# The last stage of a four-layer graph network: column sums by TensorE, squares and the row norm by ScalarE, rows in three parts, stores in five

## What is computed

```python
def _layernorm(x, axis=-1, eps=1e-05):
    m = jnp.mean(x, axis=axis, keepdims=True)
    v = jnp.var(x, axis=axis, keepdims=True)
    return (x - m) / jnp.sqrt(v + eps)
...
        agg = jax.ops.segment_sum(msg, dst, num_segments=h.shape[0])
        mean = jnp.mean(agg, axis=0)
        var = jnp.mean(jnp.square(agg - mean), axis=0)
        out = (agg - mean) * jax.lax.rsqrt(var + BN_EPS) * gamma + beta
        return out
...
    x = _layernorm(x + _L3_gnn_ref(x, L3_gnn_weight, L3_gnn_gamma, L3_gnn_beta, src, dst, edge_type_8), axis=-1)
```

## Time and profile before

| | us |
|---|---|
| three timed runs | 6064.71, 6073.38, 6078.59; median 6073.38 |
| the profiled execution: time | 6069.67 |
| its span, from the first to the last instruction | 6067.9 |
| busy in the span: PE 65%, DVE 57%, POOL 50%, PEld 50%, ACT 31% | |
| `batch_norm_out`: first VectorE instruction to the end of the span | 5971.09 to 6067.9 |

### The profile page before, as it was taken

One profiled execution on the slowest core, in us unless ns is written; L12 is line 12 of the kernel. 1 busy time (PEld: TensorE's weight loads), 2 busy tenths in 40 slices (PEclk: granted clock), 3 DMA queues, 4 the chain that ended last, 5 costly groups with the idle time before them and its releaser, 6 DMA issues. The chain is left out here.

```text
span 6067.9 us, 60178 instructions
## 1 busy us (share of the span) xinstructions
PE 3945.1 (65%) x16761; PEld 3027.2 (50%) x16761; DVE 3476.9 (57%) x6672; ACT 1868.0 (31%) x3951; POOL 3020.3 (50%) x3023
## 2 busy tenths in 40 slices
PE   1665566663966666657666667977667689945551
PEld 1564355551445555544455556855555567533331
DVE  8898544446845445466566666546666653222225
ACT  0002412213842222224445453425455443200000
POOL 3686666657763555511455552125555521066661
PEclk9656777776976777769788888988888889976776
DMA  1242244452022333333555654135556632233333
GB/s 43 62 99 51 73 116 116 114 100 52 3 45 71 100 98 97 100 71 129 156 163 172 171 163 104 38 118 169 172 165 169 158 96 79 102 96 91 94 93 48
DMA packets 281671, 630.50 MB, mean 104 GB/s; under 512 B 71500, under 2 KB 126128, under 8 KB 278192
## 3 DMA queue, kind: packets, MB, share of 16 engines
q0 software_dynamic: 159168, 436.21, 28.1%
q1 hardware_dynamic: 122224, 190.89, 10.2%
HBM read 560.35 MB, written 65.91 MB: 103 GB/s over the span
## 5 line engine op out<-in xcount | busy, mean ns | idle before, releaser
L1005 PE MATMUL edge_sums<-edge_rows,edge_hot 128*128 128x272 f32 (+2 forms) x3712 | 1182.1, 480 | 626.7 <-issue 347.0
L938 POOL DMA_INDIRECT edge_rows<-kv_rows,dst_index x928 | 879.1, 947 | 1042.0 <-PE edge_sums L1005 379.4
L1005 PEld LDWEIGHTS edge_sums<-edge_rows,edge_hot 128*128 128x128 f32 x3712 | 863.8, 241 | 882.8 <-issue 565.2
L1015 DVE TENSOR_TENSOR l_acc<-l_acc,edge_sums 128x272 f32 (+2 forms) x928 | 394.4, 425 | 557.5 <-remote 248.9
L938 POOL DMA_INDIRECT begun_rows<-xl_rows,dst_index x464 | 441.4, 951 | 434.6 <-PE edge_sums L1005 243.2
L1084 DVE TENSOR_TENSOR edge_rows<-edge_own_rows,edge_rows 128x1024 f32<-128x1024 f32 x232 | 282.6, 1218 | 545.9 <-DMA table_dst<-front_dst_stage_all 261.2
L938 POOL DMA_INDIRECT edge_rows<-rel_rows,dst_other_index x464 | 439.5, 947 | 308.2 <-issue 130.8
L1269 PE MATMUL edge_own_rows<-dst_x,edge_hot_t 128*128 x1856 | 545.3, 447 | 31.6 <-ACT edge_hot_t L969 21.2
L938 POOL DMA_INDIRECT edge_rows<-rows,src_index x464 | 439.6, 947 | 243.2 <-issue 132.7
L207 POOL DMA_INDIRECT table_src<-src_src_stage_all x333 | 415.9, 1249 | 158.0 <-issue 99.9
L1269 PEld LDWEIGHTS edge_own_rows<-dst_x,edge_hot_t 128*128 128x128 f32 x1856 | 413.8, 229 | 106.3 <-issue 34.9
(11 more groups left out here) (447 smaller groups left out, 7468.6 us busy)
## 6 DMA issues: line engine op xcount, KB each, us to landing
edge_where<-local_dst SPq DMA_DIRECT2D x174, 256.0 KB
dst_rank_keys<-in_dst SPq DMA_DIRECT2D x85, 312.5 KB
rel_rows<-nodes_out SPq DMA_DIRECT2D x25, 1024.0 KB
edge_where<-local_src SPq DMA_DIRECT2D x58, 256.0 KB
edge_rows<-kv_rows,dst_index POOLq DMA_INDIRECT x928
kv_rows<-nodes_out SPq DMA_DIRECT2D x50, 260.0 KB, 2.1
edge_rows<-rows,src_index POOLq DMA_INDIRECT x464
begun_rows<-xl_rows,dst_index POOLq DMA_INDIRECT x464
```

Of the source, the lines that this page charges most:

```text
L938: pool.indirect_dma_start(out=self.rows[:, h * U + b, 0:self.width], out_offset=None, in_=self.source[:, :], in_offset=bass.IndirectOffset ...
L1005: last = nc.tensor.matmul(sums[p % len(sums)][:, 0:width], self.hot[s % 2][:, 2 * (p % 4) + i, :], self.half(s)[:, 2 * (p % 4) + i, first: ...
L1015: nc.vector.tensor_tensor(into, into, sums[p % len(sums)][:, 0:width], ALU.add).then_inc(stored, 1)
```

## The change

Every part of `batch_norm_out` is rewritten; the rest of the program keeps its instructions and their order.

- **Sum over nodes.** VectorE adds tiles 0 to 7 and 8 to 15 into eight, then these into four tiles of `sq`. TensorE multiplies ones by tiles 16 to 24 of `acc` one by one and by those four, all 13 accumulating in one bank, `total0`.
- **Bias early.** `x + b` over all 25 tiles is done while TensorE sums; it waits for the loads of `g` and `b`.
- **Squares.** VectorE subtracts the mean five tiles at a time; ScalarE squares each five. TensorE sums 15 tiles of squares one by one, VectorE folds the last ten into five, and TensorE adds these five, 20 matmuls in `total1`.
- **Row norm in three parts** of 10, 10 and 5 tiles: scale, residual, statistics and the small sums for one part, then ScalarE's root, then reciprocal and shift. ScalarE applies `x * scale + shift` to tiles 0 to 21; VectorE does so for tiles 22 to 24.
- **Stores** of five tiles each as soon as ScalarE has counted them off; the last five go in two transfers (four tiles, 53 rows).

```diff
@@ -2476,63 +2476,131 @@
 def batch_norm_out(nc, k, acc, x, gamma, beta, out):
+    parts = [(0, 10), (10, 20), (20, NT)]
+    shared = NT - 3
     with Phase(nc, "bn") as ph:
-        norm = Norm(ph)
         g, b = ph.sb("g", [P, C]), ph.sb("b", [P, C])
         mean, scale = ph.sb("node_mean", [P, C]), ph.sb("node_scale", [P, C])
         sq = ph.sb("sq", [P, NT, C])
-        col, total = ph.sb("col", [P, C]), ph.ps("total", [P, 2, C])
+        total = [ph.ps(f"total{n}", [P, 512]) for n in range(2)]
         pad = ph.sb("pad", [P, 1])
-        own, loaded, folded, summed, varied, rooted, ready, stored = (
-            ph.sem(n) for n in ("own", "loaded", "folded", "summed", "varied", "rooted", "ready", "stored"))
+        stats = ph.sb("stats", [P, NT, 6])
+        row_mean, row_var, row_tmp, row_scale, row_shift = (ph.sb(n, [P, NT]) for n in ("row_mean", "row_var", "row_tmp", "row_scale",
+                                                                                       "row_shift"))
+        own, loaded, folded, summed, centred, squared, paired, varied, rooted, measured, spread, row_rooted, ready = (
+            ph.sem(n) for n in ("own", "loaded", "folded", "summed", "centred", "squared", "paired", "varied", "rooted",
+                                "measured", "spread", "row_rooted", "ready"))
+        added, by_act, by_dve, stored = (ph.sem(n) for n in ("added", "by_act", "by_dve", "stored"))
         block = ph.block()
+        five = lambda n: slice(5 * n, 5 * n + 5)
         @block.sync
         def _(sp):
             sp.dma_start(g[:, :], gamma.partition_broadcast(P)).then_inc(loaded, 16)
             sp.dma_start(b[:, :], beta.partition_broadcast(P)).then_inc(loaded, 16)
-            sp.wait_ge(ready, 1)
-            full = (NT - 1) * P
-            sp.dma_start(out[0:full, :].rearrange("(t p) c -> p t c", p=P), x[:, 0:NT - 1, :]).then_inc(stored, 16)
-            sp.dma_start(out[full:N, :], x[0:NL, NT - 1, :]).then_inc(stored, 16)
-            sp.wait_ge(stored, 32)
+            for n in range(NT // 5):
+                last = 5 * n + 5
+                sp.wait_ge(by_act, min(last, shared))
+                if last < NT:
+                    sp.dma_start(out[5 * n * P:last * P, :].rearrange("(t p) c -> p t c", p=P), x[:, five(n), :]).then_inc(stored, 16)
+                    continue
+                sp.wait_ge(by_dve, NT - shared)
+                sp.dma_start(out[5 * n * P:(NT - 1) * P, :].rearrange("(t p) c -> p t c", p=P), x[:, 5 * n:NT - 1, :]).then_inc(stored, 16)
+                sp.dma_start(out[(NT - 1) * P:N, :], x[0:NL, NT - 1, :]).then_inc(stored, 16)
+            sp.wait_ge(stored, 16 * (NT // 5 + 1))
         @block.tensor
         def _(pe):
-            for n in range(2):
-                pe.wait_ge(folded, n + 1)
-                nc.tensor.matmul(total[:, n, :], k.ones[:, :], col[:, :], start=True, stop=True).then_inc(summed, 1)
+            def column_sums(n, rows, start, stop):
+                for r in range(len(rows)):
+                    last = nc.tensor.matmul(total[n][:, 0:C], k.ones[:, :], rows[r], start=start and r == 0,
+                                            stop=stop and r == len(rows) - 1)
+                return last
+            column_sums(0, [acc[:, t, :] for t in range(16, NT)], True, False)
+            pe.wait_ge(folded, 1)
+            column_sums(0, [sq[:, t, :] for t in range(4)], False, True).then_inc(summed, 1)
+            for n in range(3):
+                pe.wait_ge(squared, n + 1)
+                column_sums(1, [sq[:, t, :] for t in range(5 * n, 5 * n + 5)], n == 0, False)
+            pe.wait_ge(paired, 1)
+            column_sums(1, [sq[:, t, :] for t in range(15, 20)], False, True).then_inc(summed, 1)
         @block.scalar
         def _(act):
+            for n in range(5):
+                act.wait_ge(centred, n + 1)
+                nc.scalar.activation(sq[:, five(n), :], acc[:, five(n), :], ACT.Square).then_inc(squared, 1)
             act.wait_ge(varied, 1)
             nc.scalar.activation(scale[:, :], scale[:, :], ACT.Sqrt).then_inc(rooted, 1)
-            norm.act(nc, act)
+            for n, (first, last) in enumerate(parts):
+                act.wait_ge(spread, n + 1)
+                nc.scalar.activation(row_var[:, first:last], row_var[:, first:last], ACT.Sqrt).then_inc(row_rooted, 1)
+                act.wait_ge(ready, n + 1)
+                for t in range(first, min(last, shared)):
+                    nc.scalar.activation(x[:, t, :], x[:, t, :], ACT.Identity, bias=row_shift[:, t:t + 1],
+                                         scale=row_scale[:, t:t + 1]).then_inc(by_act, 1)
         @block.vector
         def _(dve):
             step = Chain(dve, own)
-            wide = lambda a: a[:, :].unsqueeze(1).to_broadcast([P, NT, C])
-            nc.vector.tensor_reduce(col[:, :], acc[:, :, :].rearrange("p t c -> p c t"), AX.X, ALU.add).then_inc(folded, 1)
-            step(nc.vector.tensor_scalar(pad[:, :], k.row[:, :], float(NL), None, ALU.is_lt))
+            wide = lambda a, n: a[:, :].unsqueeze(1).to_broadcast([P, n, C])
+            step(nc.vector.tensor_tensor(sq[:, 0:8, :], acc[:, 0:8, :], acc[:, 8:16, :], ALU.add))
+            nc.vector.tensor_tensor(sq[:, 0:4, :], sq[:, 0:4, :], sq[:, 4:8, :], ALU.add).then_inc(folded, 1)
+            nc.vector.tensor_scalar(pad[:, :], k.row[:, :], float(NL), None, ALU.is_lt)
+            dve.wait_ge(loaded, 32)
+            nc.vector.tensor_tensor(x[:, :, :], x[:, :, :], wide(b, NT), ALU.add).then_inc(added, 1)
             dve.wait_ge(summed, 1)
-            step(nc.vector.tensor_scalar(mean[:, :], total[:, 0, :], 1.0 / N, None, ALU.mult))
-            step(nc.vector.tensor_tensor(acc[:, :, :], acc[:, :, :], wide(mean), ALU.subtract))
-
-            step(nc.vector.tensor_scalar(acc[:, NT - 1, :], acc[:, NT - 1, :], pad[:, 0:1], None, ALU.mult))
-            step(nc.vector.tensor_tensor(sq[:, :, :], acc[:, :, :], acc[:, :, :], ALU.mult))
-            nc.vector.tensor_reduce(col[:, :], sq[:, :, :].rearrange("p t c -> p c t"), AX.X, ALU.add).then_inc(folded, 1)
+            step(nc.vector.tensor_scalar(mean[:, :], total[0][:, 0:C], 1.0 / N, None, ALU.mult))
+            for n in range(5):
+                ins = nc.vector.tensor_tensor(acc[:, five(n), :], acc[:, five(n), :], wide(mean, 5), ALU.subtract)
+                if n == 4:
+                    step(ins)
+                    ins = nc.vector.tensor_scalar(acc[:, NT - 1, :], acc[:, NT - 1, :], pad[:, 0:1], None, ALU.mult)
+                ins.then_inc(centred, 1)
+            dve.wait_ge(squared, 5)
+            nc.vector.tensor_tensor(sq[:, five(3), :], sq[:, five(3), :], sq[:, five(4), :], ALU.add).then_inc(paired, 1)
             dve.wait_ge(summed, 2)
-            nc.vector.tensor_scalar(scale[:, :], total[:, 1, :], 1.0 / N, EPS, ALU.mult, ALU.add).then_inc(varied, 1)
+            nc.vector.tensor_scalar(scale[:, :], total[1][:, 0:C], 1.0 / N, EPS, ALU.mult, ALU.add).then_inc(varied, 1)
             dve.wait_ge(rooted, 1)
             step(nc.vector.reciprocal(scale[:, :], scale[:, :]))
-            dve.wait_ge(loaded, 32)
             step(nc.vector.tensor_tensor(scale[:, :], scale[:, :], g[:, :], ALU.mult))
-            step(nc.vector.tensor_tensor(acc[:, :, :], acc[:, :, :], wide(scale), ALU.mult))
-            step(nc.vector.tensor_tensor(x[:, :, :], x[:, :, :], acc[:, :, :], ALU.add))
-            step(nc.vector.tensor_tensor(x[:, :, :], x[:, :, :], wide(b), ALU.add))
-            norm.dve(nc, dve, step, x, x)
-            nc.vector.memset(pad[:, :], 0.0).then_inc(ready, 1)
+            dve.wait_ge(centred, 5)
+            def merge(n):
+                first, last = parts[n]
+                of = slice(first, last)
+                step(nc.vector.tensor_tensor(acc[:, of, :], acc[:, of, :], wide(scale, last - first), ALU.mult))
+                if not n:
+                    dve.wait_ge(added, 1)
+                step(nc.vector.tensor_tensor(x[:, of, :], x[:, of, :], acc[:, of, :], ALU.add))
+                for t in range(first, last):
+                    nc.vector.bn_stats(stats[:, t, :], x[:, t, :]).then_inc(measured, 1)
+                dve.wait_ge(measured, last)
+                nc.vector.tensor_tensor(row_mean[:, of], stats[:, of, 1], stats[:, of, 4], ALU.add)
+                nc.vector.tensor_tensor(row_tmp[:, of], stats[:, of, 1], stats[:, of, 4], ALU.subtract)
+                step(nc.vector.tensor_tensor(row_var[:, of], stats[:, of, 2], stats[:, of, 5], ALU.add))
+                nc.vector.tensor_scalar(row_mean[:, of], row_mean[:, of], 0.5, None, ALU.mult)
+                nc.vector.scalar_tensor_tensor(row_tmp[:, of], row_tmp[:, of], 0.25, row_tmp[:, of], ALU.mult, ALU.mult)
+                step(nc.vector.tensor_scalar(row_var[:, of], row_var[:, of], 1.0 / C, EPS, ALU.mult, ALU.add))
+                nc.vector.tensor_tensor(row_var[:, of], row_var[:, of], row_tmp[:, of], ALU.add).then_inc(spread, 1)
```

(13 more changed lines are left out.)

## The result

In five timed runs each the kernel before took 6068.22 us (median; 6064.71 to 6078.59) and the changed kernel 6037.86 us (6029.31 to 6042.74). That is 30.4 us less; the ratio is 0.9945, with a 95% interval of 0.9933 to 0.9957. The forecast was 6037.0 in a range of 6028 to 6050.

A forecast was written before the change was run, and what follows sets the result against it. VectorE's chain, with nothing beside it, was taken to bound the last stage. Compute 56.8 + stores 6.3 = 63.1 us against 96.8, 33.7 less, gave 6036.0 from the profiled execution, 6039.7 from the median; forecast 6037, range 6028 to 6050.

The forecast's parts named there:

- three parts: Row norm: ten, ten and five tiles cost VectorE 28.1 us together, some 4 us more than one pass.
- first sum: Sum over nodes: TensorE's 26 records take 5.7 us, free behind the bias; the mean begins at 10.4 us.
- squares: Sum of squares: TensorE, starting at 13.75 us with 3.3 us at half clock, ends last at 24.35.
- bounds of 23.7 and 31.35: End of the squares' sum in us: 23.7 with full clock at once, 31.35 with half clock throughout.
- Rival B: TensorE at half clock throughout the squares adds 7.0 us, giving 6043; chance 0.18.
- stores: End of stage: four stores go under compute, leaving 6.3 us after the last tile, against 14.0 before from issue to end.
- C: Accumulating matmuls on ones don't overlap, each costing 1.23 us: 19.6 us more, 6056; chance 0.05.
- D: The four added stores pay 2.6 us each in turn, 10.4 us, giving 6046; chance 0.06.
- E: Moved data or code slows 2320 gathers ahead of the stage; 14.5 ns each eats the gain; no change 0.03, slower 0.03.

## Why the prediction was right

| step | predicted | measured |
|---|---|---|
| mean starts | 10.4 | 10.27 |
| subtraction and zeroing done | 18.4 | 18.20 |
| VectorE's fold done | 21.3 | 21.03 |
| column scale starts | 24.35 | 25.06 |
| three parts | 28.1 | 55.85 - 28.22 = 27.6 |
| last tile normalised | 56.8 | 56.97 |
| from there to the end | 6.3 | 6.35 |
| stage | 63.1 | 63.32 |

The **first sum** was hidden behind the bias as said, at full clock, with 4.4 us to spare. That spare was in the prediction's own numbers (5.7 against 10.4) and was called cover that "was due anyway"; the run with the bias in two pieces shows that 4 us of it could have gone elsewhere. The forecast wasn't hurt, the kernel was.

The **squares** had the right last engine and a term that was 0.7 us too small: 3.3 us at half clock were assumed and 5.2 measured, which costs 0.95, while TensorE began 0.2 earlier than summed (13.57 against 13.75). The prices of 0.43 and 0.22 us a record are a little above what the earlier trace rows gives by division (2.70/7 = 0.39, 2.20/11 = 0.20); the changed kernel has 0.40 and 0.21. The bounds of 23.7 and 31.35 held, and the lower one was met by the run with the extra matmuls (23.55). Rival B, half clock throughout, did not happen in any run.

The **three parts** cost 27.6 us, 0.5 less than the sum, about 0.15 in each: the small sums took 0.9 us for 1.0, and from the root to the next part were 0.6 for 0.7. Splitting cost 3.7 us over one pass (27.63 against 23.89 in the run with one part), where some 4 were worked out. ScalarE had 0.58 us to spare ahead of the third root, where 0.8 were worked out.

The **stores** came out as summed, with the 53 rows on one engine; turning the order round confirmed the mechanism. One step was loose: the fourth store was put at 53.6 us, before the prediction's own end of part two's tiles at 54.1. It was issued at 6032.31, 54.7 us into the stage, and still left the tail as summed.

**C** (each matmul at the lone price of 1.23 us) is refuted by the 18 records in 4.12 us, 0.46 us a matmul. **D** is refuted by the run with one store. Of **E**, no sign of slower gathers was seen in the two comparisons with several runs each, and GpSimd's idle times above show none; whether anything ahead of the stage became faster is the question left open above. The times given for B, C and D were counted from the 6036 of the sum and not from the forecast of 6037.

The forecast of 6037 lay 0.9 us from the median, which is luck: the changed kernel's own runs span 13 us. What the reasoning earned is the stage.

## What to carry to other kernels

In a tail where one engine does everything, work out for each handover which engine ends last, and look at the cover from both sides: work that hides another engine's sum longer than that sum takes is path, and belongs where the first engine still waits. Look at how many DMA engines the last store moves on: here the one of 53 rows moved on a single engine, and issuing it first took 2.6 us off the end. When pieces of a change are undone one by one, lay the timelines beside each other stretch by stretch, since a sum that nearly closes can hide a piece left out and a piece counted twice. Where the whole time scatters by more than the edit is worth, compare the length of the edited stage.
